# Routing scores formed inside the local attention, batch by batch, instead of at the head of the routing stage

## The reference, cut to what matters

```python
x = x + _layernorm(_L0_attn_ref(_layernorm(x)))
norm = layer_norm(_layernorm(x), ln_g, ln_b)
scores = norm @ centroids.T                      # (8192, 8)
for e in range(E):
    s = jnp.where(taken, -jnp.inf, scores[:, e])
    _, idx = jax.lax.top_k(s, C)                 # C = 8192 // 8
```

## Time and profile before

| what | value |
|---|---|
| median of 3 runs | 2662.48 us (2655.77 to 2662.52) |
| the profiled execution, its own time | 2658.84 us |
| its span, first to last instruction | 2657.0 us |
| mean granted clock of PE | 0.896 |
| local attention | about 0 to 1020 us |
| scores of the routing | about 1020 to 1065 us |
| search for the experts' tokens and what follows | from 1065 us |
| PE, DVE, ACT, POOL busy, share of the span | 78, 75, 58, 48% |

### The profile page before, as it was taken

How to read it: one execution, slowest core, us unless ns; L and a number is a source line. 1 busy time by engine, 2 the same in 40 slices (tenths; PEclk the granted TensorE clock), 3 DMA queues, 4 the chain that set the end, 5 groups by cost and what they waited for, 6 DMA issues and landing times. The chain is left out here.

```text
span 2657.0 us, 73511 instructions
## 1 busy us (share of the span) xinstructions
PE 2064.4 (78%) x26748; PEld 1192.4 (45%) x26748; DVE 1993.9 (75%) x5359; ACT 1553.1 (58%) x2872; POOL 1283.5 (48%) x1131
## 2 busy tenths in 40 slices
PE   5999999899999987111279368888888888888687
PEld 3777777777777776000134112223222222322354
DVE  4777777777777775788458267988787888886798
ACT  4666666666666652000134146877676777777587
POOL 5777767676777660007584556423333333321122
PEclk9999999999999996555589778999898999999799
DMA  4333333333333320001223233122211112210001
GB/s 113 83 82 80 87 76 82 75 86 83 82 75 86 73 66 3 0 3 52 65 90 93 66 60 52 26 32 36 31 28 26 25 31 33 37 25 2 14 28 32
DMA packets 105849, 140.77 MB, mean 53 GB/s; under 512 B 24949, under 2 KB 80149, under 8 KB 105238
## 3 DMA queue, kind: packets, MB, share of 16 engines
q1 hardware_dynamic: 99350, 123.37, 21.6%
q0 software_dynamic: 6144, 12.60, 1.6%
HBM read 26.55 MB, written 16.78 MB: 16 GB/s over the span
## 5 line engine op out<-in xcount | busy, mean ns | idle before, releaser
L1839 DVE TENSOR_REDUCE d_nmax_<-d_s_ 128x2 bf16<-128x1024 f32 x512 | 615.0, 1223 | 142.1 <-PE d_s_ L2001 140.2
L1750 ACT ACTIVATE d_pT_<-d_t_ 128x512 f32<-128x512 f32 x1024 | 558.0, 601 | 178.9 <-PE d_t_ L2013 171.1
L282 POOL TENSOR_TENSOR a_other<-a_other,a_rope 128x512 f32<-128x512 f32 x256 | 323.9, 1286 | 290.6 <-DMA a_other<-a_raw 290.5
L2026 PE MATMUL d_o_<-d_pT_,d_v_ 128*32 128x256 f32 x4096 | 330.0, 407 | 0.2 <-ACT d_pT_ L1750 0.2
L2013 PE MATMUL d_t_<-d_qs_,d_ks_ 49*128 49x512 bf16 x1024 | 209.9, 406 | 92.5 <-ACT d_pT_ L1750 40.6
L350 ACT ACTIVATE a_pT<-a_t 64x384 f32<-64x384 f32 x512 | 247.9, 484 | 19.4 <-PE a_t L605 8.7
L2001 PE MATMUL d_s_<-d_ks_,d_qs_ 48*128 48x512 bf16 x1024 | 209.4, 405 | 18.2 <-DVE d_nmax_ L1839 13.4
L313 ACT COPY a_v<-a_proj 128x512 f32<-128x512 f32 x128 | 74.9, 585 | 235.4 <-PE a_proj L515 235.4
L2013 PEld LDWEIGHTS d_t_<-d_qs_,d_ks_ 49*128 49x128 bf16 x1024 | 49.9, 93 | 325.5 <-ACT d_pT_ L1750 212.6
L1206 ACT ACTIVATE c_hT_<-c_in_,c_beta_,c_gamma_ 128x512 f32<-128x512 f32 x16 | 12.4, 777 | 276.8 <-PE c_in_ L1326 276.8
L2026 PEld LDWEIGHTS d_o_<-d_pT_,d_v_ 128*32 128x32 f32 x4096 | 89.2, 110 | 184.6 <-ACT d_pT_ L1750 94.2
(11 more groups left out here) (268 smaller groups left out, 4872.5 us busy)
## 6 DMA issues: line engine op xcount, KB each, us to landing
a_other<-a_raw SPq DMA_DIRECT2D x512, 128.0 KB, 2.4
d_qs_<-d_part_ SPq DMA_DIRECT2D x192, 64.0 KB
d_ks_<-d_part_ SPq DMA_DIRECT2D x192, 64.0 KB
a_xpre<-x SPq DMA_DIRECT2D x16, 256.0 KB, 3.4
a_xres<-x SPq DMA_DIRECT2D x16, 256.0 KB, 3.5
c_w_<-e_w SPq DMA_DIRECT2D x16, 256.0 KB
c_xs_<-sorted_x SPq DMA_DIRECT2D x16, 256.0 KB, 2.7
sorted_x<-c_xs_ SPq DMA_DIRECT2D x16, 256.0 KB, 2.0
```

Source lines behind the costliest of these rows:

```text
L282: nc.gpsimd.tensor_tensor(other[s % 2][:, side, :], other[s % 2][:, side, :], rope[:, 1, :], ALU.mult).then_inc(rope2_done, 1)
L1750: nc.scalar.activation(pT[kt][pair][:, a, :], t_bank(j, turn)[:], ACT.Exp).then_inc(t_read, 1)
L1839: nc.vector.reduce_max(out, s_bank(unit, e)[:], AX_X, negate=True).then_inc(s_read, 1)
L2026: ins = nc.tensor.matmul(o_ps[HC * i:HC * (i + 1), cols], v[e.k][:, kt, g * GH + i, :], pT[kt][i // 2][:, i % 2, cols], start=(kt, half) = ...
```

## The change

The normalising, turning and scoring of a batch become three more parts of the attention's pipeline, at its steps 20 (DVE), 21 (PE turns, ACT applies gain and bias) and 22 (PE multiplies, ACT copies the scores to `score`, which is now a tensor that outlives the stage). The turned batch and the scores take two more uses of the two `proj` banks, placed behind `max_scores` in steps 5 and 6 of every batch from the third on. On DVE the new part stands behind `sum_statistics` and ahead of the step's last reciprocal or product, on ACT between the rounding and the exponentials. The tail is three steps longer. The routing loses its 16 groups, its ACT program, four PSUM banks and four of its seven loads. The attention loads centroids, gain and bias.

```diff
-        NLOADS = 4
+        NLOADS = 7
+        NORM_SUM, TURN_SUM, SCORE = 20, 21, 22
...
+            if s == TURN_SUM % PAIRS:
+                uses += [("zn", s)]
+            if s == SCORE % PAIRS:
+                uses += [("sc", s)]
...
-            for r in range(PAIRS + ROOT_SUM + 1):
+            for r in range(PAIRS + SCORE + 1):
...
+                if s == TURN_SUM % PAIRS and formed(b, "zn", s):
+                    use, bank = use_of(b, k, s, "zn")
+                    act.wait_ge(proj_done, use + 1)
+                    nc.scalar.activation(nT[:], proj[bank][:, 0:T], ACT.Identity, bias=beta[:],
+                                         scale=gamma[:]).then_inc(copied, 1)
+                if s == SCORE % PAIRS and formed(b, "sc", s):
+                    use, bank = use_of(b, k, s, "sc")
+                    act.wait_ge(proj_done, use + 1)
+                    nc.scalar.copy(score[:, :, bass.ds(NT * (b - 2), NT)],
+                                   proj[bank][:, 0:NT * E].rearrange("p (t e) -> p e t", e=E)).then_inc(copied, 1)
...
+            def sum_normalised(b):
+                dve.wait_ge(sum_step, b + 1)
+                for t in range(NT):
+                    ins = nc.vector.tensor_scalar(zz[:, t, :], x1[:, NT * b + t, :], mean[:, bass.ds(NT * b + t, 1)],
+                                                  comb1[:, bass.ds(NT * b + t, 1)], ALU.subtract, ALU.mult)
+                ins.then_inc(zz_ready, 1)
...
+                if s == TURN_SUM % PAIRS and formed(b, "zn", s):
+                    bank = bank_of(b, k, s, "zn")
+                    pe.wait_ge(zz_ready, b - 1)
+                    for t in range(NT):
+                        ins = nc.tensor.transpose(proj[bank][:, t * 128:(t + 1) * 128], zz[:, t, :], ident[:])
+                    ins.then_inc(proj_done, 1)
+                if s == SCORE % PAIRS and formed(b, "sc", s):
+                    bank = bank_of(b, k, s, "sc")
+                    turned_use, _ = use_of(b, k, TURN_SUM % PAIRS, "zn")
+                    pe.wait_ge(copied, turned_use + 1)
+                    for t in range(NT):
+                        ins = nc.tensor.matmul(proj[bank][:, t * E:(t + 1) * E], nT[:, t * 128:(t + 1) * 128], cent[:],
+                                               start=True, stop=True)
+                    ins.then_inc(proj_done, 1)
```

In the routing the 16 groups on DVE (`one`, `kept`), PE (`one`, `scores`) and ACT are deleted, and `NLOADS` goes from 7 to 3:

```diff
-                for u in range(G4):
-                    t = m * G4 + u
-                    ins = nc.vector.tensor_scalar(zz[k][:, u, :], x1[:, t, :], mean[:, bass.ds(t, 1)],
-                                                  comb[:, bass.ds(t, 1)], ALU.subtract, ALU.mult)
-                ins.then_inc(zz_ready, 1)
...
-            groups(dve, one)
-            for m in range(GROUPS - 2, GROUPS):
-                kept(m, m % 2)
-            dve.wait_ge(sc_kept, GROUPS)
             bits = score[:].bitcast(I32)
```

More of the change, by code:

```diff
@@ L19, with l0_attention @@
 L1_HEADS = 16
[L22 removed]
+def l0_attention(nc, x_in, w_l0, wo_l0, rope_l0, masks_q, masks_k, ident_in, x1, mean, comb1, cent_t, ln_g, ln_b, score):
     NB, T, C = x_in.shape
@@ L160, in l0_attention @@
                 uses += [("xn", s)]
+            if s == TURN_SUM % PAIRS:
+                uses += [("zn", s)]
+            if s == SCORE % PAIRS:
+                uses += [("sc", s)]
         HEAD_USES = 1 + V_AHEAD
-        assert len(uses) % 2 == 1
+        assert TURN_SUM // PAIRS == SCORE // PAIRS == 2 and len(uses) % 2 == 1
         def formed(b, what, s):
@@ L171, in formed @@
                 return b + (s >= V_FIRST) < NB
+            if what in ("zn", "sc"):
+                return 2 <= b < NB + 2
             return b < NB
-        numbered = [(b, what, s) for b in range(NB) for what, s in uses if formed(b, what, s)]
+        numbered = [(b, what, s) for b in range(NB + 2) for what, s in uses if formed(b, what, s)]
+        LEFT_OUT = 2 * sum(what in ("zn", "sc") for what, _ in uses)
         def use_of(b, k, s, what):
@@ L181, in use_of @@
             u = uses.index((what, s))
-            return HEAD_USES + len(uses) * b + u, (HEAD_USES + u + k) % 2
+            return HEAD_USES + len(uses) * b + u - LEFT_OUT, (HEAD_USES + u + k) % 2
         def use_two_back(b, s, what):
@@ L230, in _ @@
             sp.dma_start(wo_sb[:], wo_l0).then_inc(loaded, 16)
+            sp.dma_start(cent[:], cent_t).then_inc(loaded, 16)
+            sp.dma_start(gamma[:], ln_g).then_inc(loaded, 16)
+            sp.dma_start(beta[:], ln_b).then_inc(loaded, 16)
             sp.wait_ge(proj_done, 1)
@@ L486, in step @@
                     sum_statistics(batch_of(b, s, SUM_Y))
+                if due(s, NORM_SUM, before, left):
+                    sum_normalised(batch_of(b, s, NORM_SUM))
                 if s % 2 == 1 and alive(LAG_SUM, before, left):
@@ L685, in _, with routing @@
             program(pe, step)
-def routing(nc, x1, pos, pos_parts, placed, mean, comb, cent_t, ln_g, ln_b, ident_in, ones_in, before_in, spare_in, sorted_x):
+def routing(nc, x1, pos, pos_parts, placed, score, ones_in, before_in, spare_in, sorted_x):
     _, TILES, C = x1.shape
-    E = cent_t.shape[1]
+    E = score.shape[1]
     CAP = TILES * 128 // E
-    G4 = 4
     DIGITS = 8
@@ L775, in routing @@
         part_step = sem("part_step")
-        NLOADS = 7
+        NLOADS = 3
         CNT = 2 * DIGITS + 2
[L780 to L793, removed]
         block = ctx.enter_context(nc.Block())
@@ L814, in _ @@
                                         in_=x1[:, t, :], in_offset=None).then_inc(placed[0], 16)
[L816 to L827, removed]
         @block.tensor
@@ L831, in _ @@
             pe.wait_ge(loaded, 16 * NLOADS)
[L833 to L847, removed]
-                for t in range(G4):
-                    ins = nc.tensor.transpose(tp[k][:, t * 128:(t + 1) * 128], zz[k][:, t, :], ident[:])
-                ins.then_inc(zz_turned, 1)
-                if at_least(m, 1):
-                    scores(m - 1, 1 - k)
-            groups(pe, one)
-            scores(GROUPS - 1, 1)
             def ranks(flags, n):
@@ L2440, in program @@
         rstd = ctx.enter_context(nc.sbuf_tensor("rstd", [128, TILES], F32))
+        score = ctx.enter_context(nc.sbuf_tensor("score", [128, a["centroids"].shape[1], TILES], F32))
         l0_attention(nc, a["x"], a["l0_w"], a["l0_wo"], a["l0_rope"], a["l0_masks_q"], a["l0_masks_k"], a["ident"], x,
-                     mean, comb)
-        routing(nc, x, pos, pos_parts, placed, mean, comb, a["centroids"], a["ln_g"], a["ln_b"], a["ident"], a["ones"],
-                a["before"], a["spare"], sorted_x)
+                     mean, comb, a["centroids"], a["ln_g"], a["ln_b"], score)
+        routing(nc, x, pos, pos_parts, placed, score, a["ones"], a["before"], a["spare"], sorted_x)
         expert_ffn(nc, x, pos_parts[1], placed, sorted_x, a["e_w1"], a["e_b1"], a["e_w2"], a["e_b2"], a["ln_g"], a["ln_b"], a["ident"], sorted_x2)
```

34 lines of the change are left out of this document (7 added, 27 removed).

## The result

| | median | lowest to highest | runs |
|---|---|---|---|
| before | 2652.07 us | 2643.48 to 2665.24 | 10 |
| changed | 2687.49 us | 2676.39 to 2699.63 | 10 |

The ratio is 1.012, with a 95% interval of 1.0097 to 1.0142. The profiled execution of the changed kernel took 2686.03 us (span 2684.2). The forecast was 2654, and the range ended at 2670: the kernel is slower than the slow end of it. The forecast counted from a median of three runs, 2662.5; the ten runs have 2652.07, so from them the 8 us gained of the forecast lead to 2644.

A forecast was written before the change was run, and what follows sets the result against it. PE was taken to bound the attention, DVE now and then making it wait. 38.6 us gained between attention and search, less 23.5 for PE's new work and 7 for held-up normalisings, gave 8: 2662.5 to 2654 us, range 2640 to 2670.

The forecast's parts named there:

- The seam: Between attention and search: removing the routing's work saves 43.8 us, the last batch's tail costs 5.2, net 38.6 us gained.
- PE's price: Attention steps 5 and 6: turns 0.69 us plus score passes 0.99, 1.68 a batch, 23.5 us over fourteen batches.
- The rival by which PE takes the passes up: In the attention, score passes slip into idle time between weight loads, half of 23.5 us unpaid: 2640 us, chance 0.10.
- The count of catches: At step 4, DVE's four normalisings are held up by POOL's products, costing PE time, in three of fourteen batches: 7 us.
- three are of this kind, eleven like 590 or better: Batches at 287, 776 and 899 us make PE stand; in eleven, as at 590 us, the delay to DVE's normalisings hides.
- the slower rival: In the attention, DVE's normalisings meet POOL's products and DVE sets the pace: 2679 us with all caught, chance 0.11.
- The price of a catch: At step 4, PE stands 3.0 us when POOL holds up DVE's normalisings; less existing waits, 2.3 us each was counted.
- I take nothing: In the attention, PE's existing waits lie ahead of v, the new work behind it, so no absorbed time was counted.
- The turn of the loop: PE's 3.3 us wait at each turn of the attention loop; its growing with the longer body would prove the forecast wrong.
- The claim that POOL and SP are untouched: In the attention loop, SP's and POOL's instructions stay the same; no cost was counted.
- The forecast's rival with few catches: In the attention, POOL holds up DVE's normalisings in only 0 to 1 batches: 15 us gained, 2647 us, chance 0.19.
- the forecast's rival of that name: It comes to nothing: five to eight batches held up, or scores nearer half-clock price; within 3 us, 2662, chance 0.18.

The follow-up runs named there:

- the changed kernel with later uses and early powers: Changed kernel with normalising, turning and scoring one step later (21, 22, 23) and both POOL powers one step earlier (15, 18): ratio 0.9881, again 0.9883.
- the kernel before with early powers: Kernel before with both POOL powers, the output's and the sum's, one step earlier (steps 15 and 18): ratio 0.9897, again 0.9907.
- the second pair of traces: Traces from repeat runs: changed kernel, new work one step later, both POOL powers one earlier (2619.91 us); kernel before with the same earlier powers (2624.19 us).

## Why the prediction was wrong, point by point

**The seam, right.** 38.6 reckoned, 38.2 measured, with the tail at 5.4 for 5.2.

**PE's price, right.** In the changed kernel's trace the scores' rows are these:

```profile
657.05 0.34 PE L619 MATMUL a_s<-a_kB,a_qB 64*64 64x96 bf16 x16
657.33 1.06 PE L716 MATMUL a_proj<-a_cent,a_nT 128*128 128x8 f32 x8
658.31 0.36 PE L599 MATMUL a_t<-a_mk,a_identb 64*64 64x384 bf16 x4
```

From the last group of maxima to the next group behind the scores it is 1.26, without scores 0.17: 1.09 us a batch, where 0.99 was taken from the output rows' loads. The same reading with the turns gives 0.86 in ten of the fourteen batches, so 0.69 as forecast. The rival by which PE takes the passes up is dead: doubled, they lengthened the loop by about what they take.

**The count of catches, wrong.** The step "three are of this kind, eleven like 590 or better" counted gaps between POOL's instructions in a trace of before, and took it that they stay. Ten were caught. The forecast had named this as what would break it (over six catches), put the slower rival at ten, and then gave it 0.11. The normalisings alone, laid on the kernel before, took over 2 us in ten batches of fourteen: so even without PE's new work the count of three was wrong. The reason is in the rows: in thirteen of the fourteen batches of the changed kernel DVE waits for POOL's power, so it starts on POOL's mark, and the gap up to POOL's next product did not stay what it was. Before, POOL went straight on in one batch, in the changed kernel in four.

**The price of a catch, wrong in two terms.** 2.3 us each was counted. Measured, PE stood 2.8 to 4.0 us in six batches and under 1 in others. Some 2 us of it were the wait for the power, as the version with only the sum's power earlier shows. The halved clock behind a long stand was no term of the sum at all: 25 us in the body, with the share of the turns of the loop.

**The second place, missing.** "The waits of the earlier trace rows lie ahead of v, while the new work stands behind it ... I take nothing." The new work of steps 5 to 7 moved when POOL's power for the output comes against POOL's next product, and the old operation behind it was caught in six batches for 3.1 to 5.1 us, once per turn of the loop. The earlier trace rows had shown exactly this operation caught, and they were used as a price for the new one only. Freeing this place alone gives 50 us back. "I take nothing" for the waits, together with the clock that stands in no term, is the step that failed worst: the attention grew by 70 us for the 30.5 of the sum.

**The turn of the loop**, named as a risk and priced at nothing, rose from 3.3 to 4.2 us, some 4 us in five turns, and some 7 more by the clock behind them (the estimate above). With the normalisings alone it was 3.5, and 3.7 to 4.4 in each version with PE's parts.

**The claim that POOL and SP are untouched** was true of their code and wrong in effect: POOL's wait for the swap went from 204.4 us in 84 places to 249.6 in 75. Why the swap of a batch's step 0 comes late in the second batch of each turn was not settled. At 877 us POOL went from its power to the next product without a gap; at 551 us, in a batch that was not caught, it waited 3.4 us for the swap in between.

**The book, closed.** With next to nothing caught on either side, no gain of the change is shown. The medians of the changed kernel with later uses and early powers lie 4 to 6 us under those of the kernel before with early powers (2621.48 against 2627.24, and 2619.91 against 2624.19), but the runs overlap, and in the traces the keys start 4.8 and 1.6 us later, not earlier. The forecast's rival with few catches said 15 us gained. What ate them is in the second pair of traces: the seam gives 38.2 us there too, but the body is 33.6 longer (798.6 for 765.0). New work is 20.2 of it, the turns of the loop 3.8, the small stands 5.1 (12.6 for 7.5), and the clock, by the estimate from busy time at half clock (19.8 for 12.2), 3.8. That adds up to 32.9. The part of the attention outside the body takes the rest. Without the normalisings the body would be another 8 to 9 us shorter (790 for 799 and 800), half of it small stands. So, with the catches away, the change comes to nothing within the spread of the runs, and not for the reasons that the forecast's rival of that name gave. The fastest version is the changed one with later uses and early powers, 29 us (1.2%) under the kernel before; of that, 23 to 26 come from the two early powers, which the kernel before could have had.

## What to carry to other kernels

An operation that waits for another engine's result starts on that engine's mark. Where the two also hold each other up, as DVE and POOL did here, expect it to meet that engine's next instruction: a trace of before, with three such meetings counted in fourteen batches, said nothing of the ten to thirteen that came. Making the result a step earlier takes away the wait in any case, and here most of the meetings too. Work added to the pacing engine moves every such meeting: list the ones that already occur, however rare, and price each as if it came once per turn of the loop. Price a long stand of the pacing engine with the clock that it loses behind it.

## What was not expected of the hardware

A stand of PE of 5.35 us was followed by matmuls at half rate for about 4 us (0.63 for 0.39, 885.50 to 889.33), which costs 1.7 us more. In the sixteen traces, between 70 and 980 us, every stand of 3.4 us or more had such a stretch at half clock with it. Of the shorter ones some had it (1.73, 1.79, 1.92 and 2.76 us) and some not (2.06, 2.66 and 3.35), so a stand of 2 to 3 us can't be priced from its length. Doubling eight small passes per batch in one stage made PE stand 12.3 us for no visible cause in another stage, over 600 us later.
